# V of the last half projected in slot 0 alone, in a macaron block (FFN, attention, FFN) on one core

## Chip, cores and metric

One core of one Trainium2 chip. The metric is the device time of the kernel in microseconds (us), the median of the runs.

## The reference

x is 4 x 256 x 512 in float32. Three residual steps follow one another:

```python
x = x + 0.5 * ffn(layernorm(x))       # x @ W_base.T + bias, plus a rank-16 LoRA of the top 2 of 8 experts
x = x + attn(layernorm(x))            # 32 query heads, 8 KV heads of 128, RoPE, causal window of 128, then @ wo
x = x + 0.5 * ffn(layernorm(x))       # the same FFN weights again
```

In the attention q, k and v are projections of the normalised x with wq (512 x 4096), wk and wv (512 x 1024 each). The softmax runs over the keys of a window of 128.

## The kernel before, in words

Every float32 product is made of three matmuls on float32r parts: each operand is split into a "hi" part, rounded by ScalarE (ACT), and a "lo" part, the rest, computed by VectorE (DVE) or GpSimd (POOL). Most things that TensorE (PE) reads have therefore gone ACT first, DVE or POOL second.

The attention runs over 8 groups g, one for each KV head with its 4 query heads. A group has two halves hf (two of the four batches, 512 tokens), and a half has 8 slots s. In each slot one unit, a query head of one batch, goes one step down a pipeline. The order of work of a slot is written out by hand for each engine, in a function `group` in each of the four blocks (PE, ACT, DVE, POOL). Each engine runs its own list in order and waits on semaphores. Within a half this text numbers the units by their slot, 0 to 7; "unit 7 of the half before" is the last unit of the preceding half.

- PE, slot s: a piece of the projections of the half to come (`project`, L1192; m = 0 is K, 1 to 4 are the query heads, 5 is V; 12 matmuls each), the scores of unit s+1 (L1211 to L1214; they wait for the normalisation of unit s-1, which frees the score bank), the two transpositions of the probabilities of unit s-1 (L1222; they wait until the lo part of unit s-2 has been read out of the one bank they share), and in slots 1 and 5 `values` (P times V, L1235), in slots 2, 3, 6, 7 `out_project` (L1253).
- ACT, slot s: exp of unit s (L619), the hi part of V in `v_slot` (L612), the first read of a projected piece (L593 swap, or `v_copy`, L607, for V), the hi part of the probabilities of unit s-1 (`p_hi`, L627), in slots 1 and 5 the hi part of the attention output (L634).
- DVE, slot s: the normalisation of unit s (L933, L936), rope steps (L903, L894), the lo part of the probabilities of unit s-1 (`p_lo`, L943), then `v_diff` (L909) if V ended in this slot, then the row minimum of unit s+1 (`softmax_min`, L922 to L928), in slots 1 and 5 `o_lo` (L949).
- POOL: the masked copy of the probabilities (L420), the sine product and the lo part of rope (L413, L430), the lo parts of weights (L405).

V is projected transposed. When its 12 matmuls are done, `v_copy` (ACT) and `v_diff` (DVE) read the bank, `v_transpose` (PE, L1201) writes it back transposed in slot `v_slot`, and `v_hi` (ACT, L612) and `v_lo` (DVE, L914) split it.

`spread` turns a tuple of pieces for each slot into positions among the 72 matmuls of six projections, and `ended` tells in which slot a projection ends; PE, ACT, DVE and POOL all ask it. In the last group, hf = 0 projects K and the four query heads of the last half (60 matmuls), and hf = 1 projects only V (12), for itself; `v_slot` is 2 there. That half has no further half to project for, so the second FFN begins in it:

- DVE `ffn_start` (L789, L790): mean and variance of two x tiles in slot 0 and of two in slot 4, at the end of the slot; `x_lo` of tiles 0 and 1 (L812) at the end of slot 3.
- POOL `norm_rstd` in slot 1 (L395, L272 to L283, L397): 16 small steps from the variance to the scale and shift of tiles 0 and 1.
- ACT: `xn` of tiles 0 and 1 in slot 2 (L536), waits for that scale and shift; `x_hi` of the two in slot 3 (L529), behind the exp of unit 3 and `p_hi`.
- PE: `x_transpose` of tiles 0 and 1 in slot 3 (L1126), behind the scores of unit 4 and the transpositions of unit 2 and ahead of an `out_project`; from slot 4 on, six matmuls of `dense` in each slot (L1153), the first of which wait for `x_lo`.

Of the kernel before, what the change touches and what calls it, by code (L numbers as in the profile page):

```python
# [47 lines left out]

CHUNKS = (9,) * SLOTS
FIRST_HALF = (12, 12, 12, 12, 6, 6, 6, 6)  # L50
LAST_HALVES = ((8, 7, 8, 7, 8, 7, 8, 7), (6, 6, 0, 0, 0, 0, 0, 0))


def spread(first, last, hf):

    before = sum(LAST_HALVES[0]) if last and hf else 0
    chunks = LAST_HALVES[hf] if last else FIRST_HALF if first and hf == 0 else CHUNKS
    return [before + sum(chunks[:s]) for s in range(SLOTS + 1)]
# [1337 lines left out]
```

## Time and profile before

| what | value |
|---|---|
| median of 3 runs | 727.9 us (727.89 to 728.08) |
| the profiled execution, its time | 728.14 us |
| its span | 726.4 us |
| PE busy | 714.5 us, 98% of the span |
| DVE busy | 522.3 us |
| ACT busy | 424.3 us |
| POOL busy | 396.5 us |
| last half, slots 0 to 7 | about 650 to 682 us of the span |

All times below are us from the start of the span. A row of a timeline gives the start, the time, the engine, the line, the operation, what it writes and reads, how many instructions were merged, and in brackets how long the engine sat idle before it and what ended that. The matmuls overlap in the pipeline: a row's time reaches to the end of the last one, and the next may start before. On DVE and ACT too an instruction's printed time overlaps the start of the next, so the spacing of starts is what counts there.

### The profile page before, as it was taken

What the parts mean: (1) busy time and instruction counts of PE and PEld (TensorE: products, weight loads), DVE (VectorE), ACT (ScalarE), POOL (GpSimd) and SP (SyncE); (2) the same over time, 40 slices, a digit from 0 to 9 for tenths busy, and PEclk for the clock granted to TensorE, in tenths of its full rate; (3) what the DMA queues carried; (4) which work ended last, traced back from release to release, by engine and by line L of the source; (5) the groups of instructions that cost most, each with busy time, mean ns of one, the idle gap of its engine ahead of it and who ended that gap; (6) DMA issues with size and microseconds to landing.
All of it is one profiled execution on the core that took longest, in us unless ns stands there. A gap on an engine that the chain in (4) does not pass through costs nothing.

```text
span 726.4 us, 13750 instructions
## 1 busy us (share of the span) xinstructions
PE 714.5 (98%) x3699; PEld 603.5 (83%) x3699; DVE 522.3 (72%) x1773; ACT 424.3 (58%) x1146; POOL 396.5 (55%) x515
## 2 busy tenths in 40 slices
PE   8999989999999999999999999999999999999998
PEld 6887768888888888888888888888888888887886
DVE  6778776767777777677776677676767776778784
ACT  3456675556664675557655766476657665655440
POOL 2365676535853496447743765368535864374630
PEclk9999999999999999999999999999999999999999
DMA  8140013000310022002100120003000310030002
GB/s 274 56 166 29 0 39 93 15 0 8 100 40 2 0 77 68 1 1 73 58 15 1 58 73 15 1 28 103 15 2 0 102 29 0 1 117 1 0 31 88
DMA packets 25870, 32.34 MB, mean 45 GB/s; under 512 B 5834, under 2 KB 14282, under 8 KB 25300
## 3 DMA queue, kind: packets, MB, share of 16 engines
q1 hardware_dynamic: 25232, 30.69, 13.4%
q10 hardware_dynamic: 580, 1.05, 0.4%
q14 instruction: 44, 0.36, 0.2%
q8 instruction: 14, 0.23, 0.1%
HBM read 27.55 MB, written 4.19 MB: 44 GB/s over the span
## 4 chain that ended last, share of the span: by engine, by line
PE 88%; DVE 4%; POOL 4%; ACT 1%; issue 1%; DMA 1%; SPq 0%; DVEq 0%; POOLq 0%; ACTq 0%
PE bank L1192 33%; PE bank L1253 24%; PE bank L1235 8%; PE bank L1214 7%; PE bank L1153 4%; PE bank L1222 4%; PE bank L1211 2%; POOL wo_lo L405 1%; PE bank L1175 1%; PE bank L1201 1%; PE bank L1212 1%; DVE stats L789 1%; PE bank L1138 1%; PE bank L1126 1%; PE bank L1143 1%
## 5 line engine op out<-in xcount | busy, mean ns | idle before, releaser
L413 POOL TENSOR_TENSOR swap<-swap,rope 128x512 f32<-128x512 f32 x80 | 104.5, 1307 | 116.3 <-ACT swap L593 115.8
L420 POOL TENSOR_SCALAR_AFFINE_SELECT pT_hi_lo<-pT_hi_lo 128x256 fp32r<-128x256 f32 x128 | 52.4, 409 | 140.4 <-DVE pT_hi_lo L943 140.4
L619 ACT ACTIVATE bank<-sm,nmax 128x128 f32<-128x128 f32 x128 | 47.6, 372 | 105.1 <-DVE nmax L928 105.0
L627 ACT ACTIVATE pT_hi_lo<-bank 128x256 fp32r<-128x256 f32 x128 | 49.2, 385 | 95.1 <-PE bank L1222 62.8
L593 ACT ACTIVATE swap<-bank 64x512 f32<-64x512 f32 x160 | 95.1, 594 | 15.0 <-PE bank L1192 12.5
L943 DVE TENSOR_TENSOR pT_hi_lo<-bank,pT_hi_lo 128x256 fp32r<-128x256 f32 x128 | 53.8, 420 | 52.5 <-ACT pT_hi_lo L627 52.2
L430 POOL TENSOR_TENSOR q_lo<-rot,q_hi 128x512 fp32r<-128x512 f32 x64 | 82.7, 1293 | 1.3 <-ACT q_hi L601 1.3
L1253 PE MATMUL bank<-wo_hi,oT_hi 128*128 128x512 f32 x256 | 74.6, 413 | 0.0
L1192 PE MATMUL bank<-xnT_lo,wq_hi 128*128 128x512 f32 x256 | 73.3, 389 | 0.0
L894 DVE TENSOR_TENSOR rot<-bank,rope 128x512 f32<-128x512 f32 x80 | 55.1, 689 | 25.2 <-ACT swap L593 25.1
L1192 PE MATMUL bank<-xnT_hi,wq_hi 128*128 128x512 f32 x256 | 71.9, 393 | 1.0 <-DVE v_lo L914 0.8
L1192 PE MATMUL bank<-xnT_hi,wq_lo 128*128 128x512 f32 x256 | 72.2, 394 | 0.0
L903 DVE TENSOR_TENSOR rot<-rot,swap 128x512 f32<-128x512 f32 x80 | 66.8, 836 | 6.5 <-POOL swap L413 6.3
L1253 PE MATMUL bank<-wo_lo,oT_hi 128*128 128x512 f32 x256 | 68.7, 390 | 1.7 <-POOL wo_lo L405 1.7
L1253 PE MATMUL bank<-wo_hi,oT_lo 128*128 128x512 f32 x256 | 68.6, 390 | 0.0
L1235 PE MATMUL bank<-pT_hi_lo,v_hi 128*128 128x512 f32 x192 | 62.1, 404 | 0.0
L1253 PEld LDWEIGHTS bank<-wo_lo,oT_hi 128*128 128x128 f32 x256 | 47.9, 188 | 12.7 <-POOL wo_lo L405 2.5
L936 DVE TENSOR_TENSOR prob<-bank,rinv 128x256 f32<-128x256 f32 x128 | 54.4, 425 | 5.1 <-DVE rinv L933 0.3
L1214 PE MATMUL bank<-k_hi_lo,q_hi 128*128 128x256 f32 x256 | 57.7, 308 | 0.0
L1192 PEld LDWEIGHTS bank<-xnT_hi,wq_hi 128*128 128x128 f32 x256 | 47.5, 188 | 11.7 <-DVE v_lo L914 1.0
L1253 PEld LDWEIGHTS bank<-wo_hi,oT_lo 128*128 128x128 f32 x256 | 48.1, 188 | 10.1
L1192 PEld LDWEIGHTS bank<-xnT_lo,wq_hi 128*128 128x128 f32 x256 | 48.0, 188 | 10.1
(158 smaller groups left out, 1695.2 us busy)
## 6 DMA issues: line engine op xcount, KB each, us to landing
raw<-in_L_attn_wq SPq DMA_DIRECT2D x32, 256.0 KB, 2.9
raw<-in_L_attn_wo SPq DMA_DIRECT2D x32, 256.0 KB, 2.7
x<-in_L_attn_x SPq DMA_DIRECT2D x4, 512.0 KB, 7.4
raw<-in_L_attn_wk SPq DMA_DIRECT2D x8, 256.0 KB, 2.6
raw<-in_L_attn_wv SPq DMA_DIRECT2D x8, 256.0 KB, 2.6
out<-x SPq DMA_DIRECT2D x8, 256.0 KB, 2.0
raw<-in_L_ffn_W_base ACTq DMA_DIRECT2D x4, 256.0 KB, 5.3
wb_keep_hi<-q_hi SPq DMA_DIRECT2D x1, 1024.0 KB, 4.9
```

Source lines behind the costliest of these rows:

```text
L413: nc.gpsimd.tensor_tensor(w, w, tab, ALU.mult).then_inc(t2_done, 1)
L420: nc.gpsimd.affine_select(pT_both[:, :, 2, h, :], pT_both[:, :, 1, h, :].bitcast(F32), pattern=[[0, 2], [1, P]], compare_op=ALU.is_ge, fil ...
L430: nc.gpsimd.tensor_tensor(lo, rot[:, m % 2, :], hi.bitcast(F32), ALU.subtract).then_inc(qlo_done, 1)
L593: last = nc.scalar.activation(swap[a:a + half, m % 2, :], A[m % 2][b:b + half, :], ACT.Copy)
L894: nc.vector.tensor_tensor(rot[:, m % 2, :].rearrange("p (b s) -> p b s", b=2), A[m % 2][:, :].rearrange("p (b s) -> p b s", b=2), rope[:, ...
L903: nc.vector.tensor_tensor(rot[:, m % 2, :], rot[:, m % 2, :], swap[:, m % 2, :], ALU.add).then_inc(sum_done, 1)
L936: nc.vector.tensor_tensor(prob[:, s % 2, 0:2 * P].rearrange("p (c n) -> p c n", c=2), S[s % 2][:, 0:2 * P].rearrange("p (c n) -> p c n", c=2),
L943: nc.vector.tensor_tensor(pT[1][:, 0:2, s % G, :], T[:, 0:2 * P].rearrange("p (c n) -> p c n", c=2), pT[0][:, 0:2, s % G, :].bitcast(F32), ...
L1192: last = mm(A[m % 2][:, :], w, xnT[b][:, d, hf * HALF:(hf + 1) * HALF], start=(i == 0), stop=(i == 11))
L1214: last = mm(S[s % 2][:, 2 * P:4 * P], q[a][:, hf, h, q1], k[c][:, hf, b * SEQ:(b + 1) * SEQ], start=(n == 0), stop=(n == 2))
L1235: last = mm(O[i][:, :], v[a][:, par, 2 * b + kb, :], pT[c][:, blk, :, :], start=(n == 0), stop=(n == len(todo) - 1))
L1253: last = mm(wo_bank(beta, i)[:, :], oT[a][:, par, i, h, :], wo_s[c][:, h, :], start=(h == 0 and n == 0), stop=(h == G - 1 and n == 2))
```

## The change

One tuple: the half that projects only V does all twelve matmuls of it in slot 0, and none in slot 1.

```diff
 CHUNKS = (9,) * SLOTS
 FIRST_HALF = (12, 12, 12, 12, 6, 6, 6, 6)
-LAST_HALVES = ((8, 7, 8, 7, 8, 7, 8, 7), (6, 6, 0, 0, 0, 0, 0, 0))
+LAST_HALVES = ((8, 7, 8, 7, 8, 7, 8, 7), (12, 0, 0, 0, 0, 0, 0, 0))
```

As `ended` is computed from the same tuple, `v_copy` on ACT and `v_diff` on DVE move from slot 1 to slot 0 of that half. `v_transpose`, `v_hi` and `v_lo` stay in slot 2. The number of instructions is the same.

## Rows read from the trace of the kernel before

**Rows 1.** The page: the chain that ended last, shares of the span by engine.

```profile
PE 88%; DVE 4%; POOL 4%; ACT 1%; issue 1%; DMA 1%; SPq 0%; DVEq 0%; POOLq 0%; ACTq 0%
```

**Rows 2.** Waits of PE from 640 us on: in total, times, longest.

```profile
PE bank L1201 <- DVE swap L909: 1.3, 1, 1.3
PE bank L1253 <- POOL wo_lo L405: 0.5, 1, 0.5
```

**Rows 3.** Timeline of PE, slots 0 to 2 of the last half.

```profile
649.99 1.07 PE L1192 MATMUL bank<-xnT_hi,wv_hi 128*128 128x512 f32 x4
...
651.35 0.28 PE L1211 MATMUL bank<-k_hi_lo,q_hi 128*128 128x256 f32 x1
...
651.93 0.38 PE L1222 MATMUL bank<-ident,prob 128*128 128x128 f32 x2
...
654.25 0.71 PE L1235 MATMUL bank<-pT_hi_lo,v_hi 128*128 128x512 f32 x2
...
656.16 0.39 PE L1235 MATMUL bank<-pT_hi_lo,v_lo 128*128 128x512 f32 x1
657.88 0.66 PE L1201 MATMUL bank<-ident,swap 128*128 128x128 f32 x4 [1.32 <-DVE swap L909]
658.29 0.36 PE L1211 MATMUL bank<-k_hi_lo,q_hi 128*128 128x256 f32 x1
```

**Rows 4.** Timeline of ACT, slots 0 to 3 of the last half.

```profile
652.35 0.39 ACT L627 ACTIVATE pT_hi_lo<-bank 128x256 fp32r<-128x256 f32 x1 [1.63 <-PE bank L1222]
...
656.65 0.38 ACT L627 ACTIVATE pT_hi_lo<-bank 128x256 fp32r<-128x256 f32 x1 [1.36 <-PE bank L1235]
...
660.43 1.53 ACT L536 ACTIVATE swap<-x,shift,rstd 128x512 f32<-128x512 f32 x2
662.43 0.37 ACT L619 ACTIVATE bank<-sm,nmax 128x128 f32<-128x128 f32 x1 [0.47 <-DVE nmax L928]
```

**Rows 5.** Timeline of DVE, slots 0 and 1 of the last half.

```profile
652.77 0.42 DVE L943 TENSOR_TENSOR pT_hi_lo<-bank,pT_hi_lo 128x256 fp32r<-128x256 f32 x1 [0.76 <-ACT pT_hi_lo L627]
653.11 0.28 DVE L922 TENSOR_TENSOR sm<-bank,mask 128x128 f32<-128x128 f32 x1
...
655.57 0.18 DVE L790 BATCH_NORM_AGGREGATE mv<-stats 128x2 f32<-128x6 f32 x1
...
655.83 0.42 DVE L936 TENSOR_TENSOR prob<-bank,rinv 128x256 f32<-128x256 f32 x1
657.07 0.42 DVE L943 TENSOR_TENSOR pT_hi_lo<-bank,pT_hi_lo 128x256 fp32r<-128x256 f32 x1 [0.81 <-ACT pT_hi_lo L627]
657.41 0.41 DVE L909 TENSOR_TENSOR swap<-bank,swap 128x256 f32<-128x256 f32 x1
657.74 0.28 DVE L922 TENSOR_TENSOR sm<-bank,mask 128x128 f32<-128x128 f32 x1
```

**Rows 6.** Timelines of DVE and PE in the first group: a wait for p_lo.

```profile
97.48 0.41 DVE L943 TENSOR_TENSOR pT_hi_lo<-bank,pT_hi_lo 128x256 fp32r<-128x256 f32 x1
...
98.04 0.41 PE L1222 MATMUL bank<-ident,prob 128*128 128x128 f32 x2 [0.79 <-DVE pT_hi_lo L943]
```

**Rows 7.** Timeline of POOL: the first and last of the 16 steps of norm_rstd.

```profile
655.84 0.23 POOL L395 TENSOR_SCALAR shift<-mv 128x2 f32<-128x2 f32 x1 [0.80 <-DVE mv L790]
...
660.06 0.20 POOL L397 TENSOR_TENSOR shift<-shift,rstd 128x2 f32<-128x2 f32 x1
```

**Rows 8.** Timelines of DVE and PE, slot 3 and the start of slot 4.

```profile
663.30 0.17 DVE L933 RECIPROCAL rinv<-rsum 128x2 f32<-128x2 f32 x1 [0.31 <-ACT bank L619]
...
665.12 1.28 DVE L812 TENSOR_TENSOR xnT_lo<-bank,xnT_hi 128x512 fp32r<-128x512 f32 x2
...
662.73 1.04 PE L1126 MATMUL bank<-ident,swap 128*128 128x128 f32 x8
663.53 1.17 PE L1253 MATMUL bank<-wo_hi,oT_hi 128*128 128x512 f32 x4
...
666.54 1.17 PE L1153 MATMUL bank<-q_hi,xnT_hi 128*128 128x512 f32 x4
```

## Prediction

> **What bounds the kernel.** I read the page first: PE carries 88% of the chain that ended last [rows 1]. So a change pays only by the PE idle time that it removes, and costs by what it adds. Next the waits of PE from 640 us to the end. There are two, and one of them, 1.3 us, is the V transposition waiting for v_diff [rows 2]. Nothing else stops PE in the last 86 us by more than a few tenths, so whatever PE gains or loses in the last half reaches the end undiminished. Then the timelines of the four engines over slots 0 to 4 of that half, to see who stands behind whom.
>
> The gap: the last of the nine matmuls of `values` starts at 656.16; one takes about 0.23, so PE could go on at 656.39, and the V transposition starts at 657.88 [rows 3]. The gap is 1.49 (the profile prints 1.32, from the modelled end). V itself had long been projected. v_diff stands on DVE behind p_lo of unit 0 (657.07, then 657.41) [rows 5], and that one behind its p_hi on ACT, which `values` released at 656.65 [rows 4]. The gap is one of order.
>
> **The change part by part.** It removes no work and adds none: twelve V matmuls, one v_copy, one v_diff remain. No DMA and no POOL or SP instruction changes its place. Four things move.
>
> (1) PE, slot 0, is longer by six matmuls. The six that are there start at 649.99 and the scores behind them at 651.35: 1.36 or, with the rounding, 1.37 [rows 3]. The transpositions of unit 7 of the half before start at 651.93 + 1.37 = 653.30. Slot 1 loses the same six, so PE work as such sums to nothing.
>
> (2) p_hi of that unit follows its transposition: 652.35 [rows 4] + 1.37 = 653.72. v_copy now stands before it on ACT; it waits for V's end (about 652.9) and takes less than 0.4, so it is over before 653.72 and costs nothing. Without that cover p_hi would be late by at most v_copy's 0.4. p_lo: 652.77 + 1.37 = 654.14, to 654.56 [rows 5].
>
> (3) v_diff is now on DVE behind that p_lo and ahead of the row minimum of unit 1. Its spacing is 0.33 (657.41 to 657.74) [rows 5]. So the minimum starts at 653.11 + 1.37 + 0.33 = 654.81, 1.70 later, and everything behind it in slot 0 is 1.70 late: the statistics of x tiles 0 and 1 end at 655.75 + 1.70 = 657.45, the normalisation of unit 1 has its product at 655.83 + 1.70 = 657.53 and ends at 657.95 [rows 5]. DVE idled 0.76 before p_lo, but that idle time was a wait for PE and does not shrink.
>
> (4) The V transposition no longer waits for v_diff (over at about 654.9).
>
> Now who waits. **Slot 1 on PE.** Scores of unit 2 follow at 653.30 + 0.14 and take 0.58 (from 651.35 to 651.93, in slot 0) [rows 3], so the transpositions of unit 0 could start at 654.02. They must wait until p_lo of unit 7 has emptied the bank. In the first group the same wait is seen: p_lo ends at 97.89, PE starts at 98.04, 0.15 later [rows 6]. So they start at 654.56 + 0.15 = 654.71, `values` 0.17 later at 654.88, its last matmul 1.91 after that as before, and the V transposition at 654.88 + 1.91 + 0.23 = 657.02. That is 0.86 earlier than 657.88: the new wait of 0.7 has taken nearly half of the gap.
>
> **Slot 2.** The scores of unit 3 follow the V transposition by 0.41 (657.88 to 658.29) [rows 3], that is at 657.43. They need the normalisation of unit 1, which ends at 657.95: start 658.10, a wait of 0.67. Before, they started at 658.29. Of 1.49 only 0.19 is left. The next row minimum (unit 2) starts behind p_lo of unit 0. That one now follows the normalisation of unit 1 at 657.53 + 0.34 = 657.87 and the minimum at 658.20, against 657.74 before, 0.46 late [rows 5]; the out_project of slot 2 has about a microsecond to spare on it. PE reaches the x transpositions of slot 3 at 662.73 - 0.19 = 662.54 [rows 8].
>
> **The x path.** The statistics are 1.70 late and POOL's 16 steps start when they end (655.75, first step 655.84) and take 4.4 [rows 7]. xn on ACT started at 660.43, 0.17 after the last step's end and 0.13 behind what ACT's own order allowed: it was bound by POOL. So xn starts at 662.13 and its second tile ends at 663.66 instead of 661.96 [rows 4]. PE waits for it: the second set of four transpositions starts at about 663.8 and out_project at 664.2 instead of 663.53 [rows 8], 0.67 late.
>
> Behind xn on ACT stands the exp of unit 3. It started at 662.43, when the minimum was ready, after 0.47 of printed idle time [rows 4]. Instructions of ACT overlap by about 0.1 when nothing stands between them, so ACT could have begun at about 661.87: 0.56 of slack. Exp starts at 661.87 + 1.70 = 663.57, 1.14 late (the minimum, 0.46 late, is ready at 662.9). From there DVE's chain of slot 3 follows at fixed spacing: the normalisation of unit 3 at 663.30 + 1.14, p_lo, the minimum of unit 4, and x_lo from 665.12 + 1.14 = 666.26 to 667.54 [rows 8]. `dense` in slot 4 began at 666.54, 0.14 behind x_lo's end at 666.40, and so begins at 667.68. PE by its own order would be there at about 667.0, so it is x_lo that decides.
>
> **Sum.** -1.49 (the gap) + 0.63 (wait for p_lo) + 0.67 (wait for the normalisation) = -0.19 to slot 2, then +0.86 for xn less 0.19 of old wait before `dense` that goes, then +0.66 for x_lo: **+1.14 us**. From `dense` on every engine is late by 1.0 to 1.14 and PE leads, so this stays to the end. The profiled execution would have 728.14 + 1.14 = 729.3; it stands 0.24 above the median, so the median would be 727.9 + 1.1 = **729.0 us**, 0.16% more. No price here is unseen; the least sure are the hand-offs (0.05 to 0.17 each, some six in the chain), which give the sum +-0.4.
>
> A rule speaks for another result. The Trainium skill (Perfetto Trace Analysis, Optimization Strategy) says to find the gaps on the most contended engine, see what blocks them, and make those dependencies start sooner. The change does just that to the longest gap here, and by the rule the sum would be the first rival's.
>
> **Rivals.**
>
> A, the gap is simply gained, -1.5, 726.4 us. For it: 1.3 us is the longest wait of PE in this part [rows 2], and DVE and ACT are idle 0.76 and 1.63 in slot 0 [rows 4, 5]. Against it: that idle time is waiting for PE's own transpositions, which move back by 1.37. It decides in slot 1: if the transpositions of unit 0 start at about 654.0, A holds. Chance 0.05.
>
> B, the two new waits come as computed but the x path is hidden, so that -0.2 or a little less or more is left: 727.7 us. It decides at xn: should POOL's steps start earlier than I have them, or xn end by 662.5, PE is not stopped in slot 3. Against it: xn was already bound by POOL and starts only 2.3 before PE needs it. Chance 0.14. It would be the case on the other side, not slower.
>
> C, the slack of 0.56 on ACT is not there: the exp of unit 3 and x_lo are late by the whole 1.70, or a further wait of that size stands in slot 3 (x_hi behind transpositions that are themselves late): 727.9 + 1.7 = 729.6 us, slower by over 0.2%. It decides at x_lo: end at 668.1 instead of 667.5. Chance 0.21.
>
> D, it does nothing, since V's pieces only change places with as much cover: 727.9 us. Against it: slot 1 has no other filler. Chance 0.02.
>
> **Numbers.** My forecast has 0.58. A measurement can tell about 0.2%, 1.46 us, from no change. Faster by more: A, 0.05. Slower by more: C and the upper edge of my own, 0.22. Within: 0.73. The range, 727.5 to 729.8, reaches from B to C.
>
> **What would show it.** In the profile after: V's twelve matmuls in one run of 2.7 in slot 0; no idle PE before the V transposition but new waits, before L1222 on p_lo in slot 1 (about 0.6) and before the scores of slot 2 on the normalisation (about 0.5 to 0.7); v_diff in slot 0 and the statistics over at 657.4; xn at 662.1; PE idle before L1126 on ACT (about 0.5, then again between the tiles); `dense` at about 667.7 behind x_lo. Wrong would be: statistics not late by 1.7, xn not behind POOL, or a PE that comes to `dense` before 666.6.

## The result and the profile after

The changed kernel takes 729.09 us, the kernel before 727.91 us (medians of 20 runs each). The ratio is 1.0015, 95% interval 1.0009 to 1.0021: slower by about 1.2 us, less than the 0.2% named in the prediction but clear of no change. The forecast was 729.0.

The profiled execution has a span of 727.4 us against 726.4. PE's busy time is the same to a tenth, 714.5 us: no work was added, only waiting. The waits of PE from 640 us on, in total, times and longest, answer to [rows 2]:

```profile
PE bank L1153 <- DVE xnT_lo L812: 0.5, 1, 0.5
PE bank L1211 <- DVE prob L936: 0.5, 1, 0.5
PE bank L1253 <- POOL wo_lo L405: 0.5, 1, 0.5
PE bank L1222 <- DVE pT_hi_lo L943: 0.4, 1, 0.4
PE bank L1126 <- issue: 0.3, 1, 0.3
```

The one wait of 1.3 before the V transposition (L1201) is gone, and four shorter ones have taken its place, 1.79 in all by the rows of the timeline. Their places are in PE's timeline of slots 0 to 4 (to be read beside [rows 3] and the PE rows of [rows 8]):

```profile
649.87 1.07 PE L1192 MATMUL bank<-xnT_hi,wv_hi 128*128 128x512 f32 x4
...
653.17 0.38 PE L1222 MATMUL bank<-ident,prob 128*128 128x128 f32 x2
...
654.58 0.41 PE L1222 MATMUL bank<-ident,prob 128*128 128x128 f32 x2 [0.44 <-DVE pT_hi_lo L943]
...
656.90 0.60 PE L1201 MATMUL bank<-ident,swap 128*128 128x128 f32 x4
657.97 0.36 PE L1211 MATMUL bank<-k_hi_lo,q_hi 128*128 128x256 f32 x1 [0.47 <-DVE prob L936]
...
662.90 1.31 PE L1126 MATMUL bank<-ident,swap 128*128 128x128 f32 x8 [0.35 <-issue]
663.98 1.17 PE L1253 MATMUL bank<-wo_hi,oT_hi 128*128 128x512 f32 x4
...
667.51 1.17 PE L1153 MATMUL bank<-q_hi,xnT_hi 128*128 128x512 f32 x4 [0.53 <-DVE xnT_lo L812]
```

V now begins at 649.87 instead of 649.99, because PE came to the last half 0.12 earlier in this execution; that has nothing to do with the change. So the distance from V's first matmul to the first of `dense` is the measure used from here on. It was 666.54 - 649.99 = 16.55 [rows 3, 8] and is 667.51 - 649.87 = 17.64: 1.09 more. (The printed waits add up to only 0.47 more than the 1.32 of before. They do not show all the time lost, since a row's printed end reaches over the start of the next.) The eight x transpositions, printed as 1.04 before, have stretched to 1.31: the second tile was waited for. The profile names no releaser for the 0.35 before them, but it has the weight load of that line wait 0.3 for xn (L536), and the wait is gone in the first experiment below, where xn comes earlier.

DVE, slot 0 and the start of slot 1, beside [rows 5]:

```profile
654.01 0.42 DVE L943 TENSOR_TENSOR pT_hi_lo<-bank,pT_hi_lo 128x256 fp32r<-128x256 f32 x1 [2.12 <-ACT pT_hi_lo L627]
654.35 0.42 DVE L909 TENSOR_TENSOR swap<-bank,swap 128x256 f32<-128x256 f32 x1
654.68 0.28 DVE L922 TENSOR_TENSOR sm<-bank,mask 128x128 f32<-128x128 f32 x1
...
657.13 0.18 DVE L790 BATCH_NORM_AGGREGATE mv<-stats 128x2 f32<-128x6 f32 x1
...
657.40 0.42 DVE L936 TENSOR_TENSOR prob<-bank,rinv 128x256 f32<-128x256 f32 x1
```

DVE's idle time before p_lo has grown from 0.76 to 2.12 by exactly the 1.36 of the six matmuls. Behind it stand v_diff and then everything else of the slot. The statistics end at 657.31 against 655.75, 1.56 later on the clock and 1.68 later counted from V.

POOL's first and last step, and ACT from slot 2 to 3, beside [rows 7] and [rows 4]:

```profile
657.40 0.23 POOL L395 TENSOR_SCALAR shift<-mv 128x2 f32<-128x2 f32 x1 [1.13 <-DVE mv L790]
...
661.62 0.20 POOL L397 TENSOR_TENSOR shift<-shift,rstd 128x2 f32<-128x2 f32 x1
```

```profile
661.99 1.52 ACT L536 ACTIVATE swap<-x,shift,rstd 128x512 f32<-128x512 f32 x2 [1.26 <-POOL shift L397]
663.42 0.35 ACT L619 ACTIVATE bank<-sm,nmax 128x128 f32<-128x128 f32 x1
```

xn now visibly waits 1.26 for POOL. The exp of unit 3 has no idle time before it, where it had 0.47 waiting for its minimum: ACT's queue, not the softmax, decides when it starts. The chain that ended last says the same. Over these slots before, it ran through PE but for the 1.3 at the gap. Now it leaves PE in slot 0 and comes back only at `dense` (pieces in order of time: start, time, what):

```profile
650.03 2.72 PE bank L1192 x12
...
653.59 0.39 ACT pT_hi_lo L627
...
654.35 0.42 DVE swap L909
...
657.13 0.19 DVE mv L790
657.40 0.24 POOL shift L395
...
661.62 0.20 POOL shift L397
661.99 0.80 ACT swap L536
...
663.42 0.83 ACT bank L619 x4
...
666.17 1.21 DVE xnT_lo L812 x2
...
667.51 1.62 PE bank L1153 x6
```

### The profile page after: what moved, and what is told of

Its sections match the earlier page's. It is cut to its first block, busy times and chain, and to the rows that moved or that the text cites. A ratio compares the mean times of both kernels' runs of the same rounds, so it can differ in the third digit from the quotient of the medians.

```text
span 727.4 us, 13750 instructions
## 1 busy us (share of the span) xinstructions
PE 714.5 (98%) x3699; PEld 603.0 (83%) x3699; DVE 522.0 (72%) x1773; ACT 424.0 (58%) x1146; POOL 396.5 (55%) x515
## 4 chain that ended last, share of the span: by engine, by line
PE 87%; DVE 5%; POOL 4%; ACT 2%; issue 2%; DMA 1%; SPq 0%; ACTq 0%; POOLq 0%; DVEq 0%
PE bank L1192 33%; PE bank L1253 23%; PE bank L1235 8%; PE bank L1214 7%; PE bank L1153 4%; PE bank L1222 4%; PE bank L1211 2%; POOL wo_lo L405 1%; PE bank L1175 1%; DVE stats L789 1%; PE bank L1212 1%; PE bank L1201 1%; PE bank L1138 1%; DVE xnT_lo L812 1%; PE bank L1143 1%
```

## The experiments

Two theories were set against each other. Theory X: the loss is set by the x path (statistics, POOL's steps, xn, the exp of unit 3 behind it, x_lo, `dense`). Theory P, the rival: it is set by what PE waits for in slots 1 and 2, and the x path is hidden. "Before" was run beside every kernel and had a median of 727.92 each time. The changed kernel was not run again beside them: where a time is said to be less than that of the changed kernel, its 729.09 from above is meant, which had the kernel before beside it at 727.91. The ratios and intervals below are all against the kernel before. Such an interval is about 0.65 us to either side, so differences of 0.3 to 0.8 us between two medians are not settled by the intervals; the rows of the traces have to carry the argument.

### The x path shortened, after and before

On the changed kernel and on the one before, the same edit. It leaves out two of the three Newton steps of the scale of x tiles 0 and 1 in the second FFN.

```diff
-        def rstd_steps(engine, then, t0, t1):
+        def rstd_steps(engine, then, t0, t1, newton=NEWTON):
...
-            for _ in range(NEWTON):
+            for _ in range(newton):
...
-                rstd_steps(nc.gpsimd, then, t0, t1)
+                rstd_steps(nc.gpsimd, then, t0, t1, 1 if (ln, t0) == (2, 0) else NEWTON)
```

> The changed kernel, with POOL's scale and shift of x tiles 0 and 1 after one Newton step in place of three (two steps, eight small POOL operations of about 0.28 us, are left out there, so these two tiles are normalised less exactly). Nothing in slots 0 to 2 of PE, ACT or DVE is touched. Theory X (the x path sets the loss: statistics, POOL, xn, exp of unit 3 behind xn, x_lo): POOL's steps end 2.2 us earlier, xn starts at about 660.6, the exp of unit 3 is bound by its minimum again, dense starts about 0.66 earlier: 728.4 us. Theory P (what PE waits for in slots 1 and 2 sets the loss): no change, 729.1 us.

Measured: 728.35 us, 0.74 less than the changed kernel, ratio 1.0007 (0.9998 to 1.0016). Ten of the eleven runs lie between 728.15 and 728.49, below the fastest of the changed kernel (728.77). ACT and PE of this kernel:

```profile
660.47 1.52 ACT L536 ACTIVATE swap<-x,shift,rstd 128x512 f32<-128x512 f32 x2
662.61 0.37 ACT L619 ACTIVATE bank<-sm,nmax 128x128 f32<-128x128 f32 x1 [0.63 <-DVE nmax L928]
```

```profile
649.72 1.07 PE L1192 MATMUL bank<-xnT_hi,wv_hi 128*128 128x512 f32 x4
...
657.82 0.36 PE L1211 MATMUL bank<-k_hi_lo,q_hi 128*128 128x256 f32 x1 [0.46 <-DVE prob L936]
...
666.73 1.17 PE L1153 MATMUL bank<-q_hi,xnT_hi 128*128 128x512 f32 x4 [0.41 <-DVE xnT_lo L812]
```

The wait in slot 2 is as it was on the changed kernel (0.46, and 0.4 before L1222), yet `dense` comes 17.01 after V instead of 17.64. The exp waits for its minimum again. Theory P allowed no change.

This does not give back the whole loss. `dense` still comes 0.46 later than before the change (17.01 against 16.55), and so does the exp of unit 3, 12.89 after V against 12.44, now bound by its minimum. The prediction had computed that minimum to be 0.46 late. So a second chain, the softmax on DVE behind the same late normalisation of unit 1, reaches `x_lo` close behind the x path: it would cost 0.46 by itself, and the x path the further 0.63. Neither theory as worded above names it.

> A control: the kernel before with the same one Newton step in place of three on POOL for x tiles 0 and 1 (eight small operations left out, these tiles normalised less exactly). Theory X: there the exp of unit 3 is bound by its minimum and ACT has 0.56 of slack behind xn, so the 2.2 us taken off POOL are worth nothing: 727.9 us. If the gain seen on the changed kernel (0.7) came from less POOL work as such and not from the path, it comes here too: 727.2 us.

Measured: 727.96 us, ratio 0.9999 (0.9990 to 1.0008), and PE's timeline agrees with before to 0.02 up to `dense`, which starts at 666.54 in both. So less work on POOL is worth nothing here as such. ACT shows where the shorter path went:

```profile
660.28 1.52 ACT L536 ACTIVATE swap<-x,shift,rstd 128x512 f32<-128x512 f32 x2
662.43 0.37 ACT L619 ACTIVATE bank<-sm,nmax 128x128 f32<-128x128 f32 x1 [0.63 <-DVE nmax L928]
```

xn starts 0.15 earlier, bound now by ACT's own order, and the exp starts when it did. The path had slack before the change and has none after it.

### The gap removed without moving a matmul

On the kernel before:

```diff
+                        if m == 5 and last and hf == 1:
+                            v_diff(target(g, last, hf))
                         if not (start and s == 0):
                             p_lo(u - 1, s - 1)
-                        if m == 5:
+                        if m == 5 and not (last and hf == 1):
                             v_diff(target(g, last, hf))
```

> The kernel before, with v_diff in slot 1 of the last half ahead of p_lo on DVE instead of behind it. PE's order is untouched. It removes the gap before the V transposition without moving a matmul: the transposition starts near 656.8 instead of 657.9. Theory X: the statistics, POOL and xn stay where they were, so the exp of unit 3 starts only 0.33 earlier (ACT comes free of xn at 661.87) and dense only 0.33: 727.6 us; PE now waits before the x transpositions or before dense for about 0.8. Theory P: the whole 1.1 of the gap reaches the end: 726.8 us.

Measured: 727.64 us, ratio 0.9996 (0.9987 to 1.0005). PE (line numbers are two higher in this kernel):

```profile
649.93 1.07 PE L1194 MATMUL bank<-xnT_hi,wv_hi 128*128 128x512 f32 x4
...
656.58 0.66 PE L1203 MATMUL bank<-ident,swap 128*128 128x128 f32 x4
...
661.41 1.16 PE L1128 MATMUL bank<-ident,swap 128*128 128x128 f32 x8
662.75 1.17 PE L1255 MATMUL bank<-wo_hi,oT_hi 128*128 128x512 f32 x4 [0.17 <-DVE x L956]
...
666.15 1.17 PE L1155 MATMUL bank<-q_hi,xnT_hi 128*128 128x512 f32 x4 [0.39 <-DVE xnT_lo L812]
```

Counted from V, the transposition is 1.24 earlier (6.65 after V's first matmul against 7.89) and the x transpositions 1.26 (11.48 against 12.74), but `dense` only 0.33. The gain is handed back in two places: 0.54 by the start of the out_project of slot 3 (12.82 against 13.54, so 0.72 is left; the x transpositions are stretched to 1.16 and the out_project waits for an add on DVE) and 0.39 before `dense`.

What holds x_lo in this kernel is the softmax chain on DVE, not POOL and xn. The exp of unit 3 still waits for its minimum:

```profile
662.04 0.37 ACT L619 ACTIVATE bank<-sm,nmax 128x128 f32<-128x128 f32 x1 [0.18 <-DVE nmax L928]
```

That minimum comes 0.33 earlier, which is what v_diff no longer takes ahead of it. The run thus refutes theory P, but it does not show that statistics and POOL are what limits the kernel before.

So of the 1.3 that the profile showed as a wait of PE, about 0.3 was ever to be had in this way. Theory P, 726.8, is out by 0.8.

### Other work in front of the wait for x_lo

```diff
-                        if last and hf == 1 and s >= 4:
-                            if s == 4:
-                                pe.wait_ge(refetched, 32)
-                                pe.wait_ge(xlo_done, 2 * NT + 2)
+                        if last and hf == 1 and s > 4:
                             dense(1, 0, 6 * (s - 4), 6 * (s - 3))
...
                             p_transpose(u - 1, s - 1)
+                        if last and hf == 1 and s == 4:
+                            pe.wait_ge(refetched, 32)
+                            pe.wait_ge(xlo_done, 2 * NT + 2)
+                            dense(1, 0, 0, 6)
```

> The changed kernel, with the first six dense matmuls of slot 4 behind that slot's scores and transpositions instead of ahead of them. Theory X: PE has 0.70 of work that does not need x_lo to put in front, the wait before dense (0.70 from the natural start at 666.81 to 667.51) is filled and 0.7 comes back: 728.4 us. Theory P: x_lo does not matter, 729.1 us.

> The kernel before with the first six dense matmuls of slot 4 behind that slot's scores and transpositions, and nothing else. Theory X: only the 0.19 that PE lost before dense comes back: 727.7 us. If the order were good in itself, as much as on the changed kernel (0.8) comes: 727.1 us.

> The kernel before, with v_diff ahead of p_lo in slot 1 of the last half, and the first six dense matmuls of slot 4 behind that slot's scores and transpositions. Theory X: PE is about 1.0 earlier when it comes to slot 4, and 0.7 of work that needs no x_lo now stands ahead of dense, so x_lo (0.33 earlier) is just in time: dense at about 666.2 behind 0.7 more work, 726.9 us. Theory P: the gap alone, 726.8 us.

Measured: 728.28 us on the changed kernel (0.81 less), 727.62 on the one before (0.3 less), and 727.03 with v_diff first, ratio 0.9986 (0.9977 to 0.9996). On the first two the remedy is worth 0.11 more than PE was losing before `dense` (0.70 and 0.19). The expectation for the third did not set the theories apart (726.9 against 726.8). In the last one only two waits of PE are left from 640 us on:

```profile
PE bank L1255 <- POOL wo_lo L405: 0.5, 1, 0.5
PE bank L1255 <- DVE x L956: 0.2, 1, 0.2
```

On the kernel before, neither edit alone is told from no change by its interval, and together they are faster than both kernels, by 0.9 us and 2.1 us.

### DVE's order in slot 0 of the changed kernel

v_diff at the end of the slot:

```diff
-                        if m == 5:
+                        if m == 5 and not (last and hf == 1):
                             v_diff(target(g, last, hf))
...
                         if last and hf == 1:
                             ffn_start(s)
+                        if m == 5 and last and hf == 1:
+                            v_diff(target(g, last, hf))
```

> The changed kernel, with v_diff on DVE behind the row minimum of unit 1 and the statistics (end of slot 0) instead of ahead of them. The minimum and the statistics come 0.33 earlier, the normalisation of unit 1 where it was. Theory X: the x path is 0.33 earlier and with it dense: 728.8 us. Theory P: the scores of slot 2 wait for the same normalisation as before: 729.1 us.

Measured: 728.60 us, 0.49 less than the changed kernel, ratio 1.0010 (1.0001 to 1.0019). PE (line numbers are two higher):

```profile
649.65 1.07 PE L1194 MATMUL bank<-xnT_hi,wv_hi 128*128 128x512 f32 x4
...
657.75 0.36 PE L1213 MATMUL bank<-k_hi_lo,q_hi 128*128 128x256 f32 x1
...
666.93 1.17 PE L1155 MATMUL bank<-q_hi,xnT_hi 128*128 128x512 f32 x4 [0.53 <-DVE xnT_lo L812]
```

From V to `dense` it is 17.28, 0.36 less. This is the 0.33 that v_diff takes on DVE. It is paid on the path only because v_diff stands ahead of the row minimum and the statistics. PE gained nothing in slots 1 and 2: the V transposition now waits 0.29 for v_diff, and the scores of slot 2 start 8.10 after V, exactly as in the changed kernel. By theory P this kernel would have been no faster.

The statistics ahead of p_lo, without and with the edit to `dense` shown above (line numbers are up to three higher in these kernels):

```diff
-                if s in (0, 4):
+                if s == 4:
...
+                        if last and hf == 1 and s == 0:
+                            norm_stats(2, 0)
+                            norm_stats(2, 1)
                         if not (start and s == 0):
                             p_lo(u - 1, s - 1)
```

> The changed kernel, with the statistics of x tiles 0 and 1 on DVE ahead of p_lo in slot 0 (where DVE idles 2.12) instead of behind the row minimum. They end at about 653.6, but POOL starts its steps only after the lo part of rope, at about 656.3 instead of 657.4. Theory X: xn starts at about 660.7, the exp of unit 3 at 662.6, x_lo and dense 0.8 earlier: 728.2 us. Theory P: only the wait of the scores in slot 2 goes (0.47): 728.6 us.

> The changed kernel with both remedies, the statistics ahead of p_lo in slot 0 and dense behind the scores in slot 4. Theory X: the wait before dense (0.4 printed, 0.5 to 0.6 with the overlap) goes from the 728.3 of the statistics alone: 727.7 us. It still waits 0.4 for p_lo in slot 1, so it stays behind the kernel before with v_diff first and dense late (727.0). Theory P: 728.3 us.

Measured: 728.26 us, ratio 1.0005 (0.9996 to 1.0014), and 727.48 with `dense` late, 0.9994 (0.9985 to 1.0003). In both the wait in slot 2 for the normalisation goes as well, so the medians alone do not set the theories apart; the rows of ACT do. In the first, ACT's idle time before xn falls from 1.26 to 0.24 and the exp of unit 3 waits 0.27 for its minimum again:

```profile
660.72 1.52 ACT L536 ACTIVATE swap<-x,shift,rstd 128x512 f32<-128x512 f32 x2 [0.24 <-POOL shift L397]
662.50 0.37 ACT L619 ACTIVATE bank<-sm,nmax 128x128 f32<-128x128 f32 x1 [0.27 <-DVE nmax L928]
```

The waits of PE in the second:

```profile
PE bank L1256 <- POOL wo_lo L405: 0.5, 1, 0.5
PE bank L1225 <- DVE pT_hi_lo L943: 0.4, 1, 0.4
PE bank L1256 <- DVE x L956: 0.3, 1, 0.3
```

With the statistics and `dense` both moved, the changed split still carries the 0.4 wait for p_lo in slot 1, which the old split does not have. The kernel stays 0.45 us behind the best one with the old split. The intervals of the two overlap, but the traces have `dense` at 17.00 after V against 16.35, and of this 0.65 the V transposition already has 0.38 (7.03 against 6.65). So the wait for p_lo, part of what theory P points at, costs PE something there. How much of the 0.65 is due to the split is not shown, since the two kernels differ in DVE's order too: v_diff still stands ahead of a row minimum in slot 0 of this one. In the change as it was made this part lies under the other.

### Other splits of the twelve matmuls

The tuple of the kernel before, `(6, 6, ...)`, as `(11, 1, ...)` and `(9, 3, ...)`.

> V's matmuls as (11, 1) in slots 0 and 1. v_copy and v_diff stay in slot 1. p_lo, the minimum and the statistics of slot 0 are 1.14 late, not 1.70. Theory X: xn at 661.6, the exp of unit 3 0.58 late, dense +0.58: 728.5 us. The gap before the V transposition stays (1.49), and the transpositions of unit 0 wait 0.36 for p_lo: theory P gives 728.3 us.

> V's matmuls as (9, 3). The statistics are 0.68 late. Theory X: of the 0.56 of slack on ACT before the exp of unit 3 nothing is left, and dense is 0.12 late: 728.0 us. Theory P: no new wait, 727.9 us.

Measured: 728.41 us and 727.97 us. From V to `dense` it is 17.07 and 16.62, +0.52 and +0.07 where +0.58 and +0.12 were expected. PE and ACT with (11, 1):

```profile
657.93 0.66 PE L1201 MATMUL bank<-ident,swap 128*128 128x128 f32 x4 [1.32 <-DVE swap L909]
...
661.19 1.52 ACT L536 ACTIVATE swap<-x,shift,rstd 128x512 f32<-128x512 f32 x2 [0.74 <-POOL shift L397]
662.62 0.35 ACT L619 ACTIVATE bank<-sm,nmax 128x128 f32<-128x128 f32 x1
```

With (11, 1) the 1.32 before the V transposition is untouched and the kernel is still 0.5 slower. Not all of PE's order is untouched there: the V transposition comes 0.40 later after V, by the new wait for p_lo. By PE's own order `dense` would be 0.21 late (the last four matmuls of out_project start at 665.49 and take 0.91, so it could start at 666.40, 16.76 after V); x_lo makes it 0.52. With (9, 3) three matmuls (0.68) were moved and 0.07 was paid: the slack on ACT, 0.56 as computed, took nearly all the rest, and here too the exp of unit 3 has no idle time before it. The medians of these two alone would not separate the theories ((11, 1): 728.5 against 728.3); the missing idle time before the exp does.

## Why the prediction was right, point by point

- The 1.37 of six matmuls ahead of the transpositions of unit 7: 653.17 - 649.87 = 3.30 after V's start, against 1.94 before, so 1.36.
- v_copy free on ACT: it ended before the transposition was done, and p_hi started after 0.42 of idle time on ACT. Right.
- v_diff 0.33 ahead of the minimum, statistics 1.70 late: 1.68.
- New wait for p_lo in slot 1: V transposition 7.03 after V's start, computed 7.03 (657.02 - 649.99). Printed as 0.44; the spacing of starts shows 0.68 lost. For the waits in slot 2 and before `dense` it shows 0.66 and 0.70 where 0.47 and 0.53 are printed.
- New wait for the normalisation in slot 2: the scores at 8.10, computed 8.11.
- xn at 12.12, computed 12.14; the exp of unit 3 at 13.55, computed 13.58; `dense` at 17.64, computed 17.69. The last step, x_lo deciding over PE's own order, is shown by the wait of 0.53 before `dense` and by the experiment that put other work there.
- In the terms of the sum: the gap and the wait for p_lo as computed (-0.86 together), the normalisation 0.66 (0.67), xn 0.77 (0.86: the out_project of slot 3 came 0.57 late instead of 0.67), x_lo 0.70 (0.66). The two misses of size cancel in part, and the sum is 1.09 for 1.14.
- From `dense` on nothing was given back. The median rose by 1.18 where 1.14 was computed.
- The rule of the Trainium skill (Perfetto Trace Analysis, Optimization Strategy), to make the dependency behind a gap start sooner, would have given -1.5 here as the prediction read it. This case's trace does not agree with that as a price: the gap did go, and the time rose by 1.18. The kernel with v_diff first follows the rule more cheaply, and of 1.2 gained at the gap 0.3 reached the end.
- Rival A (the gap simply gained) fell in slot 1 as it was said it would. B fell at xn: its idle time of 1.26. C had the right path but the slack of 0.56 on ACT was there; (9, 3) shows it spent to within 0.05. D fell: the time moved.

The prediction's one loose term was the hand-offs, +-0.4. All the starts listed above came out within 0.05 of what was computed, except that out_project of slot 3, which is 0.10 off. That the median of 729.09 lies only 0.09 from the forecast is closer than this allowance could promise, and so in part luck; the path and its steps are not.

Not settled by any run: how much of the new wait for p_lo would remain with another order on ACT and DVE in slot 1. No other order there was tried.

## What to carry to other kernels

A wait of the busiest engine is not a price list: ask which other path joins that engine's order a little later, and how much slack it has, before counting a gap as a gain. Work put ahead of the producer of a long chain through other engines (here six matmuls ahead of two transpositions, with DVE, POOL and ACT behind them) is paid beyond that chain's slack, even if the busiest engine's own total stays the same. Relieve one path, and the next one may stand close behind it, as the softmax chain did here, so compute the lateness of each path that joins. And here a gap whose cause was program order was cheaper to close by moving the small late instruction (0.4 us on DVE) than by moving the work in front of it; look then for the next wait and cover it in the same edit.

## What was not expected

The timelines repeat far better than the run times: PE of the kernel before and of the one with a single Newton step agree to 0.02 us up to `dense` and to 0.05 us over the rest of this half, while the single runs of a kernel scatter by some tenths (the changed kernel ran from 728.77 to 729.40), and one run each of two other kernels stood 1.2 and 1.4 above its median. The start of the last half moves from execution to execution by up to 0.4 (V began between 649.64 and 650.06 in these traces), before any edited instruction. For a change of 1 us the distance between two instructions of one trace is the finer measure, and, both taken against the kernel before, it agreed with the medians within 0.1 in each of the eight kernels that keep `dense` in its place.
